# Expert phase: routed rows that are already normalised, results added to stored residuals, first layer in two-part weights

## The chip, the cores and the metric

One Trainium2 chip, one of its cores. The time is device microseconds for one execution of the program. The kernel before takes 1367.52 us (median of 3 runs, 1367.41 to 1367.99).

## The reference

The input `x` has 32 x 256 = 8192 tokens of 128 channels. Two sublayers follow each other. Each normalises its input (mean and variance over the channels, epsilon 1e-5, no scale), computes, normalises the result in the same way and adds it to its input.

```
x = x + layernorm(attention(layernorm(x)))       # 16 heads of 64, causal, 256 tokens, low-rank keys and values
x = x + layernorm(experts(layernorm(x)))         # 8 experts, each token to one of them

experts(f):  e     = argmax(f @ centroids.T)
             alpha = sigmoid(f . centroids[e])
             h     = (f - mean(f)) * rsqrt(var(f) + 1e-5) * gamma[e] + beta[e]
             y     = f + relu(h @ W1[e].T + b1[e]) @ W2[e].T + b2[e]     # 128 -> 512 -> 128
             out   = alpha * y + (1 - alpha) * f  =  f + alpha * (relu(...) @ W2[e].T + b2[e])
```

## The kernel before

Five engines run their own instruction lists and meet in semaphores; the order of the work on each is written out by hand.

**Attention** works in slots (`slot` and `phases`). A slot handles one pair of heads of one block of 256 tokens, 8 slots a block, 32 blocks. Matrices are kept in two parts, a high and a low one of type fp32r, and a product is three products of parts. ScalarE copies a result from PSUM as the high part, VectorE subtracts to get the low part (t, p, z). Beside the heads, slots carry steps for a whole block, by their place r = 0 to 7 in the block: for the block before, r 0 and 1 normalise the attention output and add the residual (x1), r 2 computes the statistics of x1 and its normalised form fn, r 3 turns fn, r 4 multiplies with the centroids, r 5 takes the argmax, r 6 computes each token's destination row, and r 7 scatters the rows. GpSimd does most of the block's small arithmetic. After the last block comes a drain of 16 slots (`not live(0)`), in which the last two blocks go through these steps.

**Routing.** A row in the DRAM tensor `routed_rows` has 136 numbers: x1 (128), the factor and shift that make fn from it, a second reciprocal deviation (of fn, for the experts' own normalisation), the best score, and the token's number. Every expert has its own region. In drain slot 6 SP and ScalarE each store four pads of 512 rows behind the regions (L224, in `pad`), with token numbers that lie outside the output. In drain slot 7 ScalarE multiplies the eight experts' first layer weights by gamma (L749). VectorE then computes a table: which expert and which rows each tile has.

**Experts** (`ffn_phases`, the functions `ffn_...`). 40 tiles of 256 rows, each of one expert, in a software pipeline: a prologue of 8 slots, a loop of 4 x 8, 5 slots of epilogue. For a tile, in order: SP loads the rows (`fin`); VectorE makes f (`ff`, L367) and its normalised form (`nn`, L375); TensorE turns it (L273), ScalarE copies it (`nt`, L310); TensorE multiplies by the first layer (L257, four blocks in fp32, in the profile two passes each); ScalarE adds the bias and relus two blocks (L317), VectorE two (L384); TensorE multiplies by the second layer (L283); ScalarE adds the bias (`yt`, L324); TensorE turns back (L266); VectorE forms f + alpha y (`gg`, L402) and its statistics (L408, L418); GpSimd takes the reciprocal deviation (L440, L442); VectorE normalises (`on`, L393); GpSimd adds x1 (`res`, L436) and scatters it to the output by two indirect DMAs (L446). ScalarE copies a tile's weights and biases, 1029 numbers a partition, into one of four buffers (L302) and computes exp(-score) (L305), of which VectorE makes alpha (L413, L422). A buffer of loaded rows is free again when the tile's scatters have landed.

Of the kernel before, what the change touches and what calls it, by code (L numbers as in the profile page):

```python
# [5 lines left out]
ALU = mybir.AluOpType  # L6
ACT = mybir.ActivationFunctionType
# [7 lines left out]
P = 128  # L15
# [4 lines left out]
C_RSTD = 128  # L20
C_SHIFT = 129
C_RSTD2 = 130
C_SCORE = 131
C_ID = 132
ROW = 136
# [4 lines left out]
def block_kernel(nc, x, wd_t, wup, wq_t, wo, cent_t, gamma_t, beta_t, ffn_w, out):  # L30
# [16 lines left out]
    TILES += -TILES % 8  # L47
# [4 lines left out]
    with ExitStack() as ctx:  # L52
# [6 lines left out]
        def sem(name):  # L59
# [53 lines left out]
        p_hi = sb("p_hi", [P, 2, 2, 384], F32R)  # L113
        p_lo = sb("p_lo", [P, 2, 2, 384], F32R)
# [7 lines left out]
        an = sb("an", [P, 2, P])  # L122
        pay = sb("pay", [P, 2, 2, ROW])
        st3 = sb("st3", [P, 2, 6])
        mv3 = sb("mv3", [P, 2, 2])
        ve3 = sb("ve3", [P, 2])
        w3 = sb("w3", [P, 3, 2])
        fn = sb("fn", [P, 2, P])
# [23 lines left out]
            dest_ready rows_written"""  # L152
# [3 lines left out]
        W1W = FB * P + FB  # L156
        WW = W1W + FB * P + 1
# [15 lines left out]
        fin = sb("fin", [P, FU, 2, ROW])  # L173
        ff = sb("ff", [P, FU, 2, P])
        nn = sb("nn", [P, 2, P])
        nt = sb("nt", [P, 2, T])
        wst = sb("wst", [P, 4, WW])
        assert 2 * HD == 2 * FB * T
        hid = wup_s[:].rearrange("p (b j t) -> p b j t", b=2, j=FB)
        yt = sb("yt", [P, T])  # L180
        ea = sb("ea", [P, FU, 2])
        ea1 = sb("ea1", [P, 2])
        alpha = sb("alpha", [P, FU, 2])
        gg = sb("gg", [P, 2, 2, P])
# [3 lines left out]
        gve = sb("gve", [P, 2])  # L188
        grs = sb("grs", [P, 2, 2])
        on = sb("on", [P, 2, P])  # L190
        res = sb("res", [P, 2, 2, P])
        for n in """pads_ready pad_stored ends_ready table_steps table_ready wst_ready exp_done nt_ready
            relu_a relu_d ff_done nn_ready n_tr h_done yt_done yt_ready y_tr alpha_steps g_steps gmv_ready gve_done
            grs_ready on_ready res_ready""".split():
            S[n] = sem(n)
# [10 lines left out]
        def ffn_phases(eng, slot):  # L206


            for s in range(FU):
                slot(0, 0, s, lambda lag: s >= lag)  # L210
# [5 lines left out]
            for s in range(5):  # L216
                slot(TILES, TILES // FU * 16, s, lambda lag: s < lag)
# [27 lines left out]
        def ffn_pe(pe):  # L245
            mm = nc.tensor.matmul

            def slot(m0, n0, s, live):
                if live(1):

                    pe.wait_ge(S["nt_ready"], m0 + s)
                    pe.wait_ge(S["wst_ready"], m0 + s)
# [886 lines left out]
```

## Time and profile before

| | us |
|---|---|
| median of 3 runs | 1367.52 |
| profiled execution | 1369.18 |
| its span, first to last instruction | 1366.2 |
| TensorE busy in the span | 1307.4 (96%) |
| VectorE | 1188.7 (87%) |
| ScalarE | 1082.8 (79%) |
| GpSimd | 908.9 (67%) |

The profile is of one execution. PE is TensorE's matmuls, PEld its weight loads, DVE is VectorE, ACT ScalarE, POOL GpSimd, SP SyncE; ACTq and SPq are what an engine's sequencer issues, DMAs for the most part. L12 is line 12 of the kernel. A matmul's end is modelled, so successive ones overlap in the rows and the distance of their starts is the better measure. Attention ends near 1130 us, the drain and the table at 1167, and the experts take the rest.

### The profile page before, as it was taken

The numbers are of one execution on the slowest core, as the hardware profiler recorded it, in microseconds if no ns is written. First come the engines' busy times: TensorE is split into PE (matmuls) and PEld (weight loads), VectorE is DVE, ScalarE is ACT, GpSimd is POOL, SyncE is SP. The second block draws the span as 40 slices with busy tenths as digits, with TensorE's granted clock in tenths as the row PEclk, the third lists the DMA queues.
The fourth block names the chain that finished last, engine by engine and source line by source line (L and its number), as shares of the span: only waits on it lengthen the run. The fifth ranks groups of instructions, "written<-read, shape, count | busy, mean of one in ns | idle before, by whom it ended". The sixth has DMA issues, their size and how long they took to land.

```text
span 1366.2 us, 34597 instructions
## 1 busy us (share of the span) xinstructions
PE 1307.4 (96%) x9120; PEld 1201.3 (88%) x9120; DVE 1188.7 (87%) x4712; ACT 1082.8 (79%) x3186; POOL 908.9 (67%) x1343
## 2 busy tenths in 40 slices
PE   6999999999999999999999999999999997699993
PEld 5999999999999999999999999999999996588782
DVE  4899999999999999999999999999999884699993
ACT  5988888888888888888888888888888884466661
POOL 3566666666666666666666666666666564288886
PEclk9999999999999999999999999999999998899997
DMA  5000000000000000000000000000000002122220
GB/s 211 5 9 13 12 12 12 12 12 12 12 12 12 12 12 12 12 12 12 11 9 8 11 12 12 12 12 12 12 12 8 8 10 76 42 62 59 60 61 8
DMA packets 38501, 31.83 MB, mean 23 GB/s; under 512 B 4882, under 2 KB 35734, under 8 KB 38080
## 3 DMA queue, kind: packets, MB, share of 16 engines
q1 hardware_dynamic: 31696, 21.47, 5.2%
q0 software_dynamic: 4656, 8.81, 1.9%
q10 hardware_dynamic: 2112, 1.11, 0.3%
q8 instruction: 16, 0.26, 0.1%
q14 instruction: 21, 0.17, 0.0%
HBM read 20.35 MB, written 12.07 MB: 24 GB/s over the span
## 4 chain that ended last, share of the span: by engine, by line
PE 82%; DVE 8%; issue 3%; POOL 3%; DMA 2%; ACT 1%; ACTq 0%; SPq 0%; POOLq 0%; DVEq 0%
PE psS L579 19%; PE psZU L643 13%; PE psZU L628 13%; PE psP L606 12%; PE psZU L631 7%; PE psT L595 5%; PE psT L597 4%; PE psT L596 4%; DVE ff L367 2%; DMA xin<-x 2%; DVE wup_s L384 1%; POOL out L446 1%; DVE on L393 1%; DVE gg L402 1%; PE psM L671 1%
## 5 line engine op out<-in xcount | busy, mean ns | idle before, releaser
L1097 POOL TENSOR_TENSOR prob<-prob,rinv 128x256 f32<-128x256 f32 (+1 forms) x512 | 412.9, 828 | 333.7 <-DVE rinv L858 330.4
L725 ACT ACTIVATE prob<-nscore,nmax 128x128 f32<-128x128 f32 (+1 forms) x1024 | 450.8, 445 | 3.1 <-DVE nmax L840 3.1
L840 DVE CUSTOM_DVE_ANT_0 nscore<-psS,mask 128x128 f32<-128x128 f32 (+1 forms) x1024 | 319.8, 349 | 0.2 <-PE psS L579 0.2
L697 ACT ACTIVATE t_hi<-psT 128x512 fp32r<-128x512 f32 x256 | 153.2, 598 | 151.3 <-PE psT L597 151.3
L827 DVE TENSOR_TENSOR t_lo<-psT,t_hi 128x512 fp32r<-128x512 f32 x256 | 176.5, 689 | 81.7 <-ACT t_hi L697 79.5
L849 DVE TENSOR_TENSOR p_lo<-psP,p_hi 128x768 fp32r<-128x768 f32 x256 | 243.3, 951 | 3.8 <-ACT p_hi L697 3.8
L697 ACT ACTIVATE p_hi<-psP 128x768 fp32r<-128x768 f32 x256 | 208.3, 814 | 6.3 <-PE psP L606 4.1
L606 PE MATMUL psP<-ident,prob 128*128 128x128 f32 x1536 | 209.3, 273 | 0.4 <-DVE p_lo L849 0.4
L863 DVE TENSOR_TENSOR z_lo<-psZU,z_hi 128x512 fp32r<-128x512 f32 x256 | 175.1, 684 | 28.4 <-ACT z_hi L697 14.4
L725 ACT ACTIVATION_READ_ACCUMULATOR prob<-nscore,nmax 128x1 f32 x1024 | 195.0, 190 | 0.0
L579 PE MATMUL psS<-t_lo,xt_hi 128*128 128x256 f32 (+1 forms) x512 | 194.3, 380 | 0.0
L606 PEld LDWEIGHTS psP<-ident,prob 128*128 128x128 f32 x1536 | 174.0, 141 | 0.6 <-issue 0.6
L579 PE MATMUL psS<-t_hi,xt_lo 128*128 128x256 f32 (+1 forms) x512 | 172.9, 338 | 0.0
L579 PE MATMUL psS<-t_hi,xt_hi 128*128 128x256 f32 (+1 forms) x512 | 172.6, 337 | 0.0
L595 PE MATMUL psT<-xt_hi,ab_lo 128*128 128x256 f32 x512 | 157.2, 307 | 2.0 <-DVE xt_lo L805 1.2
L697 ACT ACTIVATE z_hi<-psZU 128x512 fp32r<-128x512 f32 x256 | 148.1, 578 | 1.2 <-PE psZU L631 1.2
L643 PE MATMUL psZU<-z_hi,ab_lo 128*128 128x256 f32 x512 | 145.9, 285 | 0.0
L597 PE MATMUL psT<-xt_hi,ab_hi 128*128 128x256 f32 x512 | 143.8, 281 | 0.0
L596 PE MATMUL psT<-xt_lo,ab_hi 128*128 128x256 f32 x512 | 143.5, 280 | 0.0
L643 PE MATMUL psZU<-z_hi,ab_hi 128*128 128x256 f32 x512 | 143.4, 280 | 0.0
L643 PE MATMUL psZU<-z_lo,ab_hi 128*128 128x256 f32 x512 | 142.6, 279 | 0.0
L579 PEld LDWEIGHTS psS<-t_hi,xt_hi 128*128 128x128 f32 x512 | 96.4, 188 | 11.1
(168 smaller groups left out, 3295.7 us busy)
## 6 DMA issues: line engine op xcount, KB each, us to landing
fin<-routed_rows SPq DMA_DIRECT2D x40, 136.0 KB, 2.2
wx<-ffn_w SPq DMA_DIRECT2D x2, 2058.0 KB, 11.7
xin<-x SPq DMA_DIRECT2D x32, 128.0 KB, 2.2
xres<-x SPq DMA_DIRECT2D x32, 128.0 KB, 2.1
out<-res,fin POOLq DMA_INDIRECT x80, 2.3
routed_rows<-padr ACTq DMA_DIRECT2D x4, 272.0 KB, 4.3
routed_rows<-padr SPq DMA_DIRECT2D x4, 272.0 KB, 5.2
wup_s<-wup SPq DMA_DIRECT2D x1, 1024.0 KB, 5.0
```

Source lines behind the costliest of these rows:

```text
L579: last = mm(psQ[q], xx[:, xb, q * P:(q + 1) * P], tt[:, tb, :, 0:nk], start=(n == 0), stop=(n == 2))
L595: mm(psT[:, h, :], ab_lo[:, hh, 0, :], xt_hi[:, db, :], start=True, stop=False)
L596: mm(psT[:, h, :], ab_hi[:, hh, 0, :], xt_lo[:, db, :], start=False, stop=False)
L597: last = mm(psT[:, h, :], ab_hi[:, hh, 0, :], xt_hi[:, db, :], start=False, stop=True)
L606: last = nc.tensor.transpose(psP[:, h, k * P:(k + 1) * P], prob[:, s % 4, h, k * P:(k + 1) * P], ident[:])
L628: mm(psZ[:, :, :], xx[:, zx, 0, :], pp[:, zb, :, 0:T], start=(n == 0), stop=False, skip_group_check=True)
L643: last = mm(psU[:, 0:T], bb[:, hh, 1, :], zz[:, ub, h, :], start=(ur == 0 and h == 0 and n == 0), stop=(ur == PAIRS - 1 and h == 1 and n = ...
L697: cp = lambda o, i: nc.scalar.activation(o, i, ACT.Copy)
L725: last = nc.scalar.activation(prob[:, pb, h, a:z], nscore[:, (s - lag) % 2, h, a:z], ACT.Exp, bias=nmax[:, pb, h, q:q + 1], scale=-1.0, ac ...
L840: last = v.tensor_tensor_reduce(nscore[:, n1, h, a:z], psQ[q][:, h, :], mask[:, a:z], -1.0, -MASKED, ALU.add, ALU.min, nmax[:, p1, h, q:q ...
L849: v.tensor_tensor(p_lo[:, s % 2], psP[:, :, 0:384], p_hi[:, s % 2].bitcast(F32), ALU.subtract).then_inc(S["p_split"], 1)
L1097: last = g.tensor_tensor(pr, pr, rinv[:, p2, :, q:q + 1].broadcast_to([P, 2, z - a]), ALU.mult)
```

## The change

- A routed row has 132 numbers: the expert's normalised input (fn times its second reciprocal deviation), a gain (that deviation times alpha), an epsilon (the deviation squared times 1e-5), and the token's number. The expert phase works on results scaled by this deviation; its last normalisation takes the scaled epsilon, so the scale drops out. Alpha is computed in attention's slots (exp on ScalarE and two operations on VectorE at r 6), the multiplications are on GpSimd at r 4 and r 7.
- x1 is stored to the output by SP at r 2; the expert phase scatters only its normalised result, with an adding DMA. The addition `res` goes, and ff, nn and alpha's steps go from the expert phase. TensorE turns the loaded rows directly.
- First layer weights (times gamma) and the turned rows are in a high and a low part of type fp32r, and a block is three products. The weights are split in drain slots 1 to 8, high part on ScalarE, low part on VectorE; the eight scalings in slot 7 go. ScalarE copies each tile's two-part first layer (1024 numbers a partition), second layer (512) and biases (5) apart.
- 39 tiles instead of 40. The output normalisation, the scatter and the output side on VectorE come one slot later than before; buffers of the expert phase lie in those of attention, so its loads and copies wait for the last `z_ready`.

A line that only one of the two versions has is marked; of the old lines most stand in the functions above.

```diff
-C_RSTD = 128
-C_SHIFT = 129
-C_RSTD2 = 130
-C_SCORE = 131
-C_ID = 132
-ROW = 136
+C_GAIN = 128
+C_EPS = 129
+C_ID = 130
+ROW = 132
...
+        FIN = FU * 2 * ROW
+        fin = late[:, 0:FIN].rearrange("p (f t c) -> p f t c", f=FU, t=2)
+        gg = late[:, FIN:FIN + 4 * P].rearrange("p (b t c) -> p b t c", b=2, t=2)
+        nt_hi = sb("nt_hi", [P, 2, T], F32R)
+        nt_lo = sb("nt_lo", [P, 2, T], F32R)
+        w1 = sb("w1", [P, E, 2, FB * P], F32R)
+        w1st = p_both[:].rearrange("p m b h k -> p (m b h k)")[:, 0:4 * FB * P].rearrange(
+            "p (b m f) -> p b m f", b=2, m=2)
+        w2st = kv_t[:].rearrange("p (b m) j c -> p b (m j c)", b=2).rearrange("p b (m f) -> p (b m) f", m=2)
+        biases = sb("biases", [P, E, FB + 1])
+        bst = sb("bst", [P, 4, FB + 1])
...
+            n = TILES // FU
+            for s in range(FU):
+                slot(n * FU, n * 16, s, lambda lag: s - lag < rest)
+            for s in range(rest + 6 - FU):
+                slot((n + 1) * FU, (n + 1) * 16, s, lambda lag: s + FU - lag < rest)
...
+                    sp.wait_ge(S["z_ready"], PAIRS * NB)
...
+                    b = (s - 1) % 2
                     for j in range(FB):
-                        last = mm(psH[:, j, :], wst[:, (s - 1) % 4, j * P:(j + 1) * P], nt[:, (s - 1) % 2, :],
-                                  start=True, stop=True)
+                        for n, (m, nt) in enumerate(((1, nt_hi), (0, nt_lo), (0, nt_hi))):
+                            last = mm(psH[:, j, :], w1st[:, b, m, j * P:(j + 1) * P], nt[:, b, :],
+                                      start=(n == 0), stop=(n == 2))
...
+                    pe.wait_ge(f_loaded[s], n0 + 16)
...
+                        last = nc.tensor.transpose(psN[:, t * P:(t + 1) * P], fin[:, s, t, 0:P], ident[:])
...
+                    pe.wait_ge(S["w2st_ready"], m0 + s - 1)
...
+                if live(3):
+                    act.wait_ge(S["yt_done"], m0 + s - 2)
+                    if live(4):
+                        act.wait_ge(S["y_tr"], m0 + s - 3)
+                    nc.scalar.activation(yt[:], psY[:, 0, :], ACT.Identity,
+                                         bias=bst[:, (s - 3) % 4, FB:FB + 1]).then_inc(S["yt_ready"], 1)
                 if live(0):
-
+                    e = act.value_load(table[0:1, bass.ds(m0 + s, 1), 1], min_val=0, max_val=E - 1)
+                    if live(2):
+                        act.wait_ge(S["h_done"], m0 + s - 1)
+                    nc.scalar.activation(w1st[:, s % 2].rearrange("p m f -> p (m f)"),
+                                         w1[:, bass.ds(e, 1)].rearrange("p a m f -> p (a m f)"),
+                                         ACT.Copy).then_inc(S["w1st_ready"], 1)
+                if live(1):
+                    act.wait_ge(S["h_done"], m0 + s)
+                    act.wait_ge(S["w2st_ready"], m0 + s)
+                    if live(3):
+                        act.wait_ge(S["yt_done"], m0 + s - 2)
+                    for j in range(2):
+                        last = nc.scalar.activation(hid[:, (s - 1) % 2, j, :], psH[:, j, :], ACT.Relu,
+                                                    bias=bst[:, (s - 1) % 4, j:j + 1])
+                    last.then_inc(S["relu_a"], 1)
+                if live(0):
+                    act.wait_ge(S["n_tr"], m0 + s + 1)
+                    cp = lambda o, i: nc.scalar.activation(o, i, ACT.Copy)
+                    cp(nt_hi[:, s % 2, :], psN[:, 0:T]).then_inc(S["nt_hi_done"], 1)
...
+                    cp(w2st[:, s % 4, :], wx[:, bass.ds(e, 1), W2:W2 + FB * P].rearrange("p a c -> p (a c)"))
+                    cp(bst[:, s % 4, :], biases[:, bass.ds(e, 1), :].rearrange("p a c -> p (a c)")
+                       ).then_inc(S["w2st_ready"], 1)
...
+                if live(4):
+
+                    b, sf = s % 2, (s - 4) % FU
+                    m = m0 + s - 4
+                    dve.wait_ge(S["y_tr"], m + 1)
+                    if live(6):
+                        dve.wait_ge(S["on_ready"], m - 1)
                     for t in range(2):
...
+                        last = v.scalar_tensor_tensor(gg[:, b, t, :], psO[:, t, 0:P], fin[:, sf, t, C_GAIN:C_GAIN + 1],
+                                                      fin[:, sf, t, 0:P], ALU.mult, ALU.add)
                     last.then_inc(S["g_steps"], 1)
...
+                if live(1):
+                    dve.wait_ge(S["h_done"], m0 + s)
+                    dve.wait_ge(S["w2st_ready"], m0 + s)
...
+                    for j in range(2, FB):
+                        last = v.tensor_scalar(hid[:, (s - 1) % 2, j, :], psH[:, j, :],
+                                               bst[:, (s - 1) % 4, j:j + 1], 0.0, ALU.add, ALU.max)
...
+                if live(5):
+                    b = (s - 5) % 2
+                    dve.wait_ge(S["grs_ready"], m0 + s - 4)
+                    if live(7):
+                        dve.wait_ge(stored[(s - 7) % FU], n0 + n0 + (32 if s >= 7 else 0))
+                    for t in range(2):
+                        last = v.tensor_scalar(on[:, b, t, :], gg[:, b, t, :], gmv[:, b, t, 0:1], grs[:, b, t:t + 1],
+                                               ALU.subtract, ALU.mult)
+                    last.then_inc(S["on_ready"], 1)
...
+                    dve.wait_ge(S["nt_hi_done"], m0 + s + 1)
+                    v.tensor_tensor(nt_lo[:, s % 2, :], psN[:, 0:T], nt_hi[:, s % 2, :].bitcast(F32),
+                                    ALU.subtract).then_inc(S["nt_ready"], 1)
...
+            pool.wait_ge(S["x1_stored"], 16 * NB)
...
+                    m, b, sf = m0 + s - 4, s % 2, (s - 4) % FU
+                    pool.wait_ge(S["gmv_ready"], m + 1)
+                    g.tensor_tensor(gve[:, b, :], gmv[:, b, :, 1], fin[:, sf, :, C_EPS], ALU.add).then_inc(S["gve_done"], 1)
+                    pool.wait_ge(S["gve_done"], m + 1)
+                    g.tensor_tensor(grs[:, b, :], gve[:, b, :], neg_half[:], ALU.pow).then_inc(S["grs_ready"], 1)
+                if live(5):
+                    m, b, sf = m0 + s - 5, (s - 5) % 2, (s - 5) % FU
+                    wait_apart(pool, S["on_ready"], m + 1)
                     for t in range(2):
                         g.indirect_dma_start(out, bass.IndirectOffsetOnAxis(
-                            ap=fin[:, sf, t, C_ID:C_ID + 1].bitcast(U32), axis=0), res[:, b, t, :], None,
-                            bounds_check=ntok - 1, oob_is_err=False).then_inc(stored[sf], 16)
+                            ap=fin[:, sf, t, C_ID:C_ID + 1].bitcast(U32), axis=0), on[:, b, t, :], None,
+                            bounds_check=ntok - 1, oob_is_err=False,
+                            compute_op=ALU.add).then_inc(stored[sf], 16)
...
+                if r == 2 and live_b(2):
+                    sp.wait_ge(S["x1_ready"], b0 + db - 1)
+                    sp.dma_start(out[bass.ds((b0 + db - 2) * T, T), :].rearrange("(t p) c -> p t c", p=P),
+                                 x1[:, db]).then_inc(S["x1_stored"], 16)
...
+                if not live(0) and 1 <= s <= E:
+                    act.wait_ge(S["ffnw_loaded"], 5 * 16)
+                    nc.scalar.activation(w1[:, s - 1, 0, :], wx[:, s - 1, 0:FB * P], ACT.Copy,
+                                         scale=gam[:, s - 1:s]).then_inc(S["w1_hi_done"], 1)
...
+                if r == 6 and live_b(2):
+                    act.wait_ge(S["argmax_steps"], 3 * (b0 + db) - 5)
+                    nc.scalar.activation(ea[:], best[:], ACT.Exp, scale=-1.0).then_inc(S["exp_done"], 1)
...
-                if not live(0) and s == 7:
-
-                    act.wait_ge(S["bias_done"], E // 2 + 1)
-                    for e in range(E):
-                        last = nc.scalar.activation(wx[:, e, 0:FB * P], wx[:, e, 0:FB * P], ACT.Copy,
-                                                    scale=gam[:, e:e + 1])
-                    last.then_inc(S["weights_ready"], 1)
...
+                if not live(0) and 1 <= s <= E:
+                    dve.wait_ge(S["w1_hi_done"], s)
+                    v.scalar_tensor_tensor(w1[:, s - 1, 1, :], wx[:, s - 1, 0:FB * P], gam[:, s - 1:s],
+                                           w1[:, s - 1, 0, :].bitcast(F32), ALU.mult,
+                                           ALU.subtract).then_inc(S["w1_split"], 1)
...
-                    n = b0 + db - 1
-                    dve.wait_ge(S["r3_steps"], 6 * n - 4)
-                    v.scalar_tensor_tensor(pay[:, db, :, C_SHIFT], mv3[:, :, 0], -1.0, pay[:, db, :, C_RSTD],
-                                           ALU.mult, ALU.mult)
...
+                if r == 6 and live_b(2):
+
+                    dve.wait_ge(S["exp_done"], b0 + db - 1)
+                    v.tensor_scalar(ea1[:], ea[:], 1.0, None, ALU.add).then_inc(S["alpha_steps"], 1)
+                    dve.wait_ge(S["alpha_steps"], 2 * (b0 + db) - 3)
+                    v.reciprocal(alpha[:], ea1[:]).then_inc(S["alpha_steps"], 1)
...
+                    g.tensor_tensor(x1[:, db], an[:], xres[:, db], ALU.add).then_inc(S["x1_ready"], 1)
...
+                if r == 4 and live_b(2):
+
+                    n = b0 + db - 1
+                    wait_apart(pool, S["f_ready"], n)
+                    g.tensor_tensor(pay[:, db, :, 0:P], fn[:], rstd2[:].unsqueeze(2).broadcast_to([P, 2, P]),
+                                    ALU.mult).then_inc(S["nn_stored"], 1)
+                    g.tensor_tensor(sq2[:], rstd2[:], rstd2[:], ALU.mult).then_inc(S["gain_steps"], 1)
+                    pool.wait_ge(S["gain_steps"], 2 * n - 1)
+                    g.tensor_tensor(pay[:, db, :, C_EPS], sq2[:], eps_t[:], ALU.mult).then_inc(S["gain_steps"], 1)
...
+                    n = b0 + db - 1
+                    pool.wait_ge(S["alpha_steps"], 2 * n)
+                    g.tensor_tensor(pay[:, db, :, C_GAIN], rstd2[:], alpha[:], ALU.mult).then_inc(S["gain_ready"], 1)
+                    wait_apart(pool, S["dest_ready"], n)
+                    pool.wait_ge(S["gain_ready"], n)
+                    pool.wait_ge(S["nn_stored"], n)
+                    pool.wait_ge(S["gain_steps"], 2 * n)
```

## Rows read from the trace of the kernel before

**Rows 1.** Busy time by stretch: us, each engine's busy us (instructions), clock, DMA
```profile
60.00:1120.00 1060.00, 1059.53 (x7753) 990.28 (x7752) 959.35 (x3782) 910.14 (x2765) 713.56 (x1052) 1.00 0.04 11
1167.35:1172.13 4.78, 0.69 (x2) 0.29 (x2) 2.22 (x10) 1.49 (x3) 0.00 (x0) 0.50 0.35 89
1196.74:1336.39 139.65, 135.38 (x661) 112.28 (x660) 136.08 (x562) 90.51 (x198) 119.47 (x166) 1.00 0.20 60
```

**Rows 2.** Timeline of TensorE, experts: start us, us, what, idle before
```profile
1172.13 3.34 PE L257 MATMUL psS<-nt,wst 128*128 128x256 f32 x8 [0.47 <-ACT nt L310]
...
1272.68 1.89 PE L257 MATMUL psS<-nt,wst 128*128 128x256 f32 x8
1274.41 0.38 PE L266 MATMUL psZU<-ident,yt 128*128 128x128 f32 x2
1274.68 0.44 PE L273 MATMUL psZU<-ident,nn 128*128 128x128 f32 x2
1274.96 1.89 PE L283 MATMUL psT<-wup_s,wst 128*128 128x256 f32 x8
...
1336.39 1.89 PE L257 MATMUL psS<-nt,wst 128*128 128x256 f32 x8
```

**Rows 3.** Groups, 1196.74 to 1336.39: busy us, mean ns of one, idle before
```profile
L446 POOL DMA_INDIRECT out<-res,fin x67 | 67.2, 1003 | 17.5 <-issue 15.0 <-DVE on L393 2.4
L302 ACT ACTIVATE wst<-wx 128x1029 f32 x33 | 35.1, 1062 | 11.8 <-ACT yt L324 11.8
L384 DVE TENSOR_SCALAR wup_s<-psS,wst 128x256 f32<-128x256 f32 x66 | 28.7, 476 | 0.2
L367 DVE TENSOR_SCALAR ff<-fin 128x128 f32<-128x128 f32 x66 | 26.2, 437 | 1.0 <-issue 1.0
L436 POOL TENSOR_TENSOR res<-on,fin 128x256 f32<-128x256 f32 x33 | 24.6, 746 | 0.4
L393 DVE TENSOR_SCALAR on<-gg,gmv,grs 128x128 f32<-128x128 f32 x66 | 20.7, 366 | 0.0
L375 DVE TENSOR_SCALAR nn<-ff,fin 128x128 f32<-128x128 f32 x66 | 15.9, 283 | 1.2
```

**Rows 4.** Timeline between the phases
```profile
1146.37 0.49 DVE L785 BATCH_NORM_STATS2 st<-psM 128x6 f32<-128x128 f32 x2
1147.22 5.87 ACTq L224 DMA_DIRECT2D routed_rows<-padr  x4
...
1149.38 0.21 POOL L975 TENSOR_TENSOR ve<-mv,eps_t 128x2 f32<-128x2 f32 x1
...
1153.13 5.01 ACT L749 ACTIVATE wx<-wx,gam 128x512 f32<-128x512 f32 x8 [8.16 <-issue]
...
1158.04 0.36 ACT L697 ACTIVATE ft<-psM 128x256 f32<-128x256 f32 x1
...
1167.35 32.39 SPq L240 DMA_DIRECT2D fin<-routed_rows  x10
```

**Rows 5.** Chain of waits, attention: start us, us, what
```profile
1082.12 0.70 PE psZU L643 x6
```

**Rows 6.** Groups, 60 to 1130 us
```profile
L935 DVE SCALAR_TENSOR_TENSOR pay<-mv,pay 128x2 f32<-128x2 f32 x30 | 25.1, 836 | 0.0
L805 DVE TENSOR_TENSOR xt_lo<-psM,xt_hi 128x256 fp32r<-128x256 f32 x29 | 11.3, 391 | 0.0
```

**Rows 7.** Timeline of VectorE, attention, slot after r 6
```profile
635.91 0.69 DVE L827 TENSOR_TENSOR t_lo<-psT,t_hi 128x512 fp32r<-128x512 f32 x1 [0.28 <-ACT t_hi L697]
```

**Rows 8.** Timeline of GpSimd in the tail
```profile
1338.80 1.03 POOL L446 DMA_INDIRECT out<-res,fin  x1 [0.20 <-issue]
...
1356.92 0.98 POOL L446 DMA_INDIRECT out<-res,fin  x1 [0.30 <-issue]
```

**Rows 9.** DMA issues: number, KB each, us to landing
```profile
fin<-routed_rows SPq DMA_DIRECT2D x40, 136.0 KB, 2.2
out<-res,fin POOLq DMA_INDIRECT x80, 2.3
```

More of the change, by code:

```diff
@@ L126, in block_kernel @@
         ve3 = sb("ve3", [P, 2])
+        rs3 = sb("rs3", [P, 2])
         w3 = sb("w3", [P, 3, 2])
+        rstd2 = sb("rstd2", [P, 2])
+        sq2 = sb("sq2", [P, 2])
+        best = sb("best", [P, 2])
+        ea = sb("ea", [P, 2])
+        ea1 = sb("ea1", [P, 2])
+        alpha = sb("alpha", [P, 2])
         fn = sb("fn", [P, 2, P])
@@ L172, in block_kernel @@
         table = sb("table", [P, TILES, 2], I32)
[L173 to L178, printed above, removed]
+        late = prob[:].rearrange("p a h k -> p (a h k)")
+        FIN = FU * 2 * ROW
[9 more added lines that the diff above has]
+        bst = sb("bst", [P, 4, FB + 1])
+        assert 2 * HD == 2 * FB * T and HD // P == 2 * FB
         hid = wup_s[:].rearrange("p (b j t) -> p b j t", b=2, j=FB)
         yt = sb("yt", [P, T])
[L181 to L184, printed above, removed]
         gst = sb("gst", [P, 2, 6])
@@ L187, in block_kernel @@
         gmv = sb("gmv", [P, 2, 2, 2])
-        gve = sb("gve", [P, 2])
+        gve = sb("gve", [P, 2, 2])
         grs = sb("grs", [P, 2, 2])
[L190 to L194, printed above, removed]
+        on = sb("on", [P, 2, 2, P])
+        for n in """pads_ready pad_stored ends_ready table_steps table_ready w1_hi_done w1_split w1st_ready w2st_ready
+            nt_hi_done nt_ready relu_a relu_d n_tr h_done yt_done yt_ready y_tr g_steps gmv_ready gve_done
+            grs_ready on_ready""".split():
             S[n] = sem(n)
@@ L272, in slot @@
                     for t in range(2):
-                        last = nc.tensor.transpose(psN[:, t * P:(t + 1) * P], nn[:, t, :], ident[:])
+                        last = nc.tensor.transpose(psN[:, t * P:(t + 1) * P], fin[:, s, t, 0:P], ident[:])
                     last.then_inc(S["n_tr"], 1)
@@ L281, in slot @@
                     for j in range(FB):
-                        a = W1W + j * P
-                        last = mm(psY[:, 0, :], wst[:, (s - 2) % 4, a:a + P], hid[:, s % 2, j, :],
+                        last = mm(psY[:, 0, :], w2st[:, (s - 2) % 4, j * P:(j + 1) * P], hid[:, s % 2, j, :],
                                   start=(j == 0), stop=(j == FB - 1))
@@ L378, in slot @@
-                if live(1):
-                    dve.wait_ge(S["h_done"], m0 + s)
-                    if live(3):
-                        dve.wait_ge(S["yt_done"], m0 + s - 2)
-                    w = wst[:, (s - 1) % 4, :]
-                    for j in range(2, FB):
-                        last = v.tensor_scalar(hid[:, (s - 1) % 2, j, :], psH[:, j, :],
-                                               w[:, FB * P + j:FB * P + j + 1], 0.0, ALU.add, ALU.max)
-                    last.then_inc(S["relu_d"], 1)
@@ L387, in slot @@
-                if live(4):
-                    b = s % 2
-                    dve.wait_ge(S["grs_ready"], m0 + s - 3)
-                    if live(5):
-                        dve.wait_ge(S["res_ready"], m0 + s - 4)
-                    for t in range(2):
-                        last = v.tensor_scalar(on[:, t, :], gg[:, b, t, :], gmv[:, b, t, 0:1], grs[:, b, t:t + 1],
-                                               ALU.subtract, ALU.mult)
-                    last.then_inc(S["on_ready"], 1)
@@ L396, in slot @@
-                if live(3):
-                    b, sf = (s - 3) % 2, (s - 3) % FU
-                    m = m0 + s - 3
-                    dve.wait_ge(S["y_tr"], m + 1)
-                    for t in range(2):
-                        last = v.scalar_tensor_tensor(gg[:, b, t, :], psO[:, t, 0:P], alpha[:, sf, t:t + 1],
-                                                      ff[:, sf, t, :], ALU.mult, ALU.add)
+                if live(4):
[4 more added lines that the diff above has]
+                        dve.wait_ge(S["on_ready"], m - 1)
+                    for t in range(2):
+                        last = v.scalar_tensor_tensor(gg[:, b, t, :], psO[:, t, 0:P], fin[:, sf, t, C_GAIN:C_GAIN + 1],
+                                                      fin[:, sf, t, 0:P], ALU.mult, ALU.add)
@@ L921, in misc_early @@
                     b1v = wx[:, :, B1:W2]
-                    v.tensor_tensor(b1v, psT[:, 0, 0:E * FB].rearrange("p (e j) -> p e j", e=E), b1v,
+                    v.tensor_copy(biases[:, :, FB:FB + 1], wx[:, :, W2 + FB * P:W2 + FB * P + 1])
+                    v.tensor_tensor(biases[:, :, 0:FB], psT[:, 0, 0:E * FB].rearrange("p (e j) -> p e j", e=E), b1v,
                                     ALU.add).then_inc(S["bias_added"], 1)
```

106 lines of the change are left out of this document (22 added, 84 removed).

## The prediction

> **What bounds the kernel now.** I read the busy time by stretch first [rows 1]. Until 1120 us TensorE is busy 1059.53 of 1060.00 us: attention is TensorE's. In the steady part of the expert phase, 33 tiles from 1196.74 to 1336.39, one tile takes 139.65/33 = 4.23 us, and of it TensorE is busy 4.10, VectorE 4.12, GpSimd 3.62 and ScalarE 2.74. Three engines are near the end of the tile, so faster matmuls alone would give little. TensorE's own floor is read from one tile in which it never stopped [rows 2]: first layer 1.73 (1272.68 to 1274.41), two pairs of transposes 0.27 and 0.28, second layer 1.73, together 4.01. GpSimd's 3.62 is not all: the group of scattering DMAs shows 17.5 us of idle time before 67 of them, 0.53 a tile [rows 3], so it is bound for 4.15. Third, the timeline between the phases [rows 4]: 1142 to 1172 is a chain of small steps with TensorE nearly idle.
>
> **Steady expert tile.** First layer: eight fp32 passes in 1.73 become 12 fp32r products. Six products of this kind with changing weights take 0.70 [rows 5], so 12 x 0.118 = 1.42, and TensorE's floor falls by 0.31 to 3.70. VectorE loses ff and nn (26.2 + 15.9 us over 33 tiles, 1.28 a tile [rows 3]) and two small operations on alpha; it gains the low half of the turned rows, 0.39 by the same subtraction in attention [rows 6]: at most 4.12 - 1.28 + 0.39 = 3.23. GpSimd loses the residual addition: 4.15 - 0.75 = 3.40. ScalarE gains a copy of the second layer's weights, half of the 1029-wide copy's 1.06 [rows 3], and its exponential becomes a copy of five biases: 2.74 + 0.53 = 3.27. So TensorE becomes the floor, if the ring holds: from the start of a first layer, 1.42 + about 0.2 of release, then on VectorE two reluing halves (2 x 0.476), the two output normalisations (2 x 0.366), and the low half (0.39), which the next first layer waits for: 3.69, equal to TensorE's 3.70. ScalarE's reluing, high half and copies run beside that. I take 3.75; bounds 3.70 and 4.0 (the ring with collisions on top).
>
> **Number of tiles.** 39 instead of 40: 38 intervals between the first and the last first layer, where there were 39 in 1336.39 - 1172.13 = 164.26 [rows 2]. The granted clock is 0.50, the 1.2 GHz level, while TensorE is nearly idle before the first tile [rows 1], and the first of the intervals is stretched by that: 1.42 x 3.34/1.73 = 2.74 [rows 2], release 0.2, reluing 0.95, low half with release 0.6: 4.5. The second has no output transposes: 3.4. The others: 36 x 3.75 = 135.0. Another 1.0 for loop edges, which a TensorE without slack now pays. 143.9: **-20.4**.
>
> **Attention.** Each 256-token block gains on GpSimd one 128x256 multiply (the addition of this size is 0.746 [rows 3]) and three tiny ones, some 1.5 us where GpSimd is busy 713.56 of 1060 [rows 1]; on ScalarE one tiny exponential; on VectorE two tiny operations (some 0.3 with their waits) ahead of z_lo in slot 6 of the block, and it loses the two-input operation on L935, which shows 836 ns [rows 6]. SP gains a 128 KB store behind a wait for x1_ready that its next load waits for anyway. Against the 0.3 stands VectorE's idle 0.28 before the next t_lo [rows 7]; TensorE is the bound and has no wait there. I take 0. Bounds: -1 (some hidden waits on VectorE go) and +8 (0.25 in each of 30 blocks if that cover fails).
> L935 alone shows a mechanism: 836 ns for 128x2 elements that run beside GpSimd's normalisation. The Trainium skill (GPSIMD Engine Reference, Specifications) says that GpSimd shares its SBUF interfaces with VectorE and contends with instructions that have two SBUF inputs. By that rule the new weight split, two SBUF inputs as well, could wait once for a GpSimd operation in the drain, where VectorE has the time: the sum stays, within 0.8.
>
> **Between the phases.** Here I expect a loss. ScalarE's sequencer is held by the pad stores for 5.87 us from 1147.22 [rows 4]; until now nothing on VectorE waited for what comes behind them. Now ScalarE's seventh high-half copy (drain slot 7) is queued behind the pads, and VectorE's low half of it stands first in VectorE's slot 7, ahead of the statistics of the last attention output. Those began at 1146.37. Now: pads until 1153.1, the 512-wide copy 0.7, the split 0.7, statistics and aggregation 0.85: 1155.4. GpSimd took the result at 1149.38, since its scatter was in its way: +6.1. Behind it all is serial: GpSimd rs2, an, x1, fn, transpose. Back comes that ft was held by the eight weight scalings (ft at 1158.04, could be 1156.5): -1.5. The last block's alpha adds two operations before the table and a multiply before the last scatter: +0.8. First load of rows at 1167.35 + 5.4: **+5.4**. Bounds: -1.5 (no such wait) and +7.
>
> **Load to first layer.** 4.78 until now. ff and nn go (1.17), the low half comes (0.5): **-0.6**.
>
> **Tail.** From the start of the last first layer to the end of the last scatter it was 1357.90 - 1336.39 = 21.5 [rows 2, 8], paced by GpSimd. Now the first of five pairs of scatters is ready after 1.42 + 0.2 + 0.95 + 0.73 = 3.3, three more tiles at 3.40, then two pairs end on end at 2.5 each: 18.5. An adding scatter reads before it writes; landing is 2.3 now [rows 9], and I take 0.5 more: **-2.5**, bounds -3 and +2.
> The profile's row has plain stores only. The Trainium skill (DMA: Bandwidth & Descriptors, Rules for kernel authors) says that an accumulating DMA reads its destination and writes it later. By that rule, with the 2.2 of a load [rows 9] put on top of the 2.3, the tail alone would be 1.7 longer than in my sum, and the rows that are freed would still be in time.
> How much landing is free: the second scatter of a tile goes out some 4.5 us into its slot, and the load that reuses its rows needs 3.1, all within three slots and 1.7: up to 3 x 3.75 + 1.7 - 4.5 - 3.1 = 5.3.
>
> **Sum.** -20.4 + 5.4 - 0.6 - 2.5 = -18.1. The profiled execution took 1369.18 for a span of 1366.2; the median of the runs is 1.66 lower, so the sum is taken from the median: 1367.52 - 18.1 = **1349.4**.
>
> **Rivals.**
> A. The wait behind the pads doesn't reach the path: 1349.4 - 6.1 = 1343.3. For it: waits of several steps hide in each other there. Against: both queues are in order, and the profile shows ScalarE idle behind the pads.
> B. The steady tile stays near 4.0, as ring, ScalarE and GpSimd collide: 36 x 0.25 = +9.0, 1358.4. For it: four engines between 3.2 and 3.75 with a wait at each handing over. Against: TensorE was 4.10 busy of 4.23 with three engines as full.
> C. Attention pays 0.25 in each block: 1357.
> D. Slower: issuing the adding scatter holds GpSimd longer than the plain one's 1.0 [rows 3]. GpSimd's tile is 3.40 and grows by twice what one issue grows; TensorE's 3.75 hides 0.17 of it. The gain of 18.1 over 36 tiles is used up at a tile of 4.25, which is an issue of 1.43. At 1.6 a tile is 4.6: 36 x 0.85 + 5 in the tail = +35, 1385. For it: no row shows such a scatter. Against: the addition needs no more indices or rows.
>
> **Chances.** Forecast 0.55, A 0.10, B 0.17, C 0.08, D 0.10 (in a part of D it stays within the gain). Range: down to 1341 (A, with tiles at 3.70), up to 1361 (B with a slower landing); D is left out. A change of 0.2% (2.7 us) is what can be told from none here. Faster 0.88, within it 0.03, slower 0.09.
>
> **What would show it.** First layer: 12 products in 1.42. Steady first layers 3.7 to 3.8 apart with TensorE without idle time. VectorE's statistics in the drain at about 1155, with the low half of slot 7 waiting for ScalarE ahead of them; first load of rows near 1172.7. The adding scatter at 1.0 of GpSimd. I am wrong if that issue is over 1.2, if the steady tile is over 3.9, or if the drain's wait isn't there.

## The result: slower, 1385.84 us, and where the time went

The changed kernel takes 1385.84 us (median of 4 runs, 1384.52 to 1388.91), the kernel before 1367.76 beside it: ratio 1.0134, 95% interval 1.0115 to 1.0152. It was forecast at 1349.4, in a range up to 1361. The profiled execution took 1385.37 for a span of 1383.6.

The span grew by 17.4 us. Four stretches make it up, each between two rows that both timelines have (the first load of routed rows, the first and the last start of a first layer, the end):

| stretch | before | after | difference | forecast |
|---|---|---|---|---|
| start to first load of rows | 1167.35 | 1173.66 | +6.3 | +5.4 |
| first load to first first layer | 4.78 | 3.97 | -0.8 | -0.6 |
| first to last first layer | 164.26 | 170.77 | +6.5 | -20.4 |
| last first layer to the end | 29.8 | 35.2 | +5.4 | -2.5 |

Busy time by stretch of the kernel after, as [rows 1] (us, then each engine's busy us, granted clock, DMA share, GB/s):

```profile
60.00:1120.00 1060.00, 1058.03 (x7737) 988.94 (x7736) 955.05 (x3805) 907.74 (x2794) 743.27 (x1169) 1.00 0.05 15
1173.66:1177.63 3.97, 0.69 (x2) 0.29 (x3) 0.42 (x1) 1.71 (x3) 0.00 (x0) 0.50 0.44 96
1200.00:1340.00 140.00, 121.59 (x733) 100.57 (x733) 95.31 (x367) 99.95 (x212) 122.21 (x121) 1.00 0.42 55
```

In the expert phase VectorE has become light (95.31 of 140, where it had 136.08 of 139.65) and TensorE has idle time (121.59). GpSimd is the fullest, and its groups show that it is full to the end (busy us, mean ns of one, idle before):

```profile
L439 POOL DMA_INDIRECT out<-on,prob x61 | 95.9, 1572 | 15.7 <-issue 15.7
L432 POOL TENSOR_TENSOR gve<-gmv,prob 128x2 f32<-128x2 f32 x30 | 23.3, 778 | 0.0
```

The adding scatter holds it 1572 ns, where the plain one held it 1003 [rows 3]. With 15.7 us of "issue" (its own sequencer, nobody else) it is occupied for 122.21 + 15.7 = 137.9 of 140. One tile in GpSimd's timeline, and then the next:

```profile
1276.24 1.59 POOL L439 DMA_INDIRECT out<-on,prob  x1 [0.20 <-issue]
1278.13 1.55 POOL L439 DMA_INDIRECT out<-on,prob  x1 [0.30 <-issue]
1279.14 0.78 POOL L432 TENSOR_TENSOR gve<-gmv,prob 128x2 f32<-128x2 f32 x1
1280.00 0.72 POOL L434 TENSOR_TENSOR grs<-gve,neg_half 128x2 f32<-128x2 f32 x1
1280.91 1.59 POOL L439 DMA_INDIRECT out<-on,prob  x1 [0.20 <-issue]
```

1280.91 - 1276.24 = 4.67 us, and no other engine is waited for in it. TensorE's first layers follow at that pace, 4.64 apart on average between 1200 and 1310 us (the second to seventh interval were still 3.4 to 3.8; the first scatter goes out only at 1196.8). The waits of the others say the same only indirectly (us in total, times, longest):

```profile
DVE on L413 <- DMA out<-on,prob: 27.4, 29, 1.6
PEld psZU L285 <- DMA prob<-routed_rows: 18.0, 26, 1.0
PEld psS L269 <- DVE nt_lo L418: 12.9, 24, 1.6
```

Read alone, they accuse the landing of the scatter and the load of rows behind it. Both are possible readings, so the first experiments had to separate a slow issue (GpSimd's own time for the instruction) from a slow landing (the time until the data are written and the buffer is free).

### The profile page after: what moved, and what is told of

It reads as the page before. It is cut to its first block and busy times, and to the rows that moved or that the text cites. A ratio compares the mean times of both kernels' runs of the same rounds, so it can differ in the third digit from the quotient of the medians.

```text
span 1383.6 us, 34964 instructions
## 1 busy us (share of the span) xinstructions
PE 1296.3 (94%) x9256; PEld 1193.4 (86%) x9256; DVE 1151.7 (83%) x4541; ACT 1100.1 (80%) x3251; POOL 959.1 (69%) x1428
## 3 DMA queue, kind: packets, MB, share of 16 engines
q0 software_dynamic: 13328, 8.68, 4.5%
q10 hardware_dynamic: 2112, 1.08, 0.4%
## 5 line engine op out<-in xcount | busy, mean ns | idle before, releaser
L847 DVE TENSOR_TENSOR p_both<-psP,p_both 128x768 fp32r<-128x768 f32 x256 | 243.7, 952 | 1.2 <-ACT p_both L695 1.1
L695 ACT ACTIVATE p_both<-psP 128x768 fp32r<-128x768 f32 x256 | 208.1, 813 | 4.0 <-PE psP L604 2.4
L861 DVE TENSOR_TENSOR z_lo<-psZU,z_hi 128x512 fp32r<-128x512 f32 x256 | 174.6, 682 | 27.6 <-ACT z_hi L695 18.5
L626 PE MATMUL psZU<-p_both,xk_hi 128*128 128x512 f32 x512 | 160.7, 394 | 0.0
```

Source lines behind the costliest of these rows:

```text
L626: mm(psZ[:, :, :], xx[:, zx, 0, :], pp[:, zb, :, 0:T], start=(n == 0), stop=False, skip_group_check=True)
L695: cp = lambda o, i: nc.scalar.activation(o, i, ACT.Copy)
L847: v.tensor_tensor(p_lo[:, s % 2], psP[:, :, 0:384], p_hi[:, s % 2].bitcast(F32), ALU.subtract).then_inc(S["p_split"], 1)
L861: v.tensor_tensor(z_lo[:, (s - 5) % 2], psZ[:], z_hi[:, (s - 5) % 2].bitcast(F32), ALU.subtract).then_inc(S["z_split"], 1)
```

## The experiments

**1. The scatter without the addition.** The output then lacks the stored residuals.

```
-                            bounds_check=ntok - 1, oob_is_err=False,
-                            compute_op=ALU.add).then_inc(stored[sf], 16)
+                            bounds_check=ntok - 1, oob_is_err=False).then_inc(stored[sf], 16)
```

> The changed kernel with the last scatter storing instead of adding (the output then lacks the stored residual). Issue theory: the adding scatter holds GpSimd 1.57 us against 1.00 of the plain one, and with two of them a tile is 4.67 long on GpSimd; without it each issue is back at 1.0, GpSimd's tile at 3.5, the steady tile at TensorE's 3.7 to 3.8 and the time at 1350 (-36 from 1385.8). Landing theory (the read before the write makes the scatter land late, and the output normalisation waits for it): the same 1350, since it lands early again. If adding has nothing to do with it (the ring over VectorE is the limit, or the loads of rows): the tile stays at 4.5 to 4.7, 1380 to 1386.

1357.32 us, ratio 0.9917 (0.9899 to 0.9935). One attribute is worth 28.5 us. GpSimd's timeline with the plain scatter:

```profile
1282.95 1.04 POOL L439 DMA_INDIRECT out<-on,prob  x1 [0.19 <-issue]
1284.29 0.98 POOL L439 DMA_INDIRECT out<-on,prob  x1 [0.30 <-issue]
1285.26 0.29 POOL L432 TENSOR_TENSOR gve<-gmv,prob 128x2 f32<-128x2 f32 x1
1285.63 0.72 POOL L434 TENSOR_TENSOR grs<-gve,neg_half 128x2 f32<-128x2 f32 x1
1286.54 1.04 POOL L439 DMA_INDIRECT out<-on,prob  x1 [0.20 <-issue]
```

3.59 where nothing waits, 1.08 less than 4.67. But the tiles came on average 3.95 apart, not at 3.7 to 3.8, and the time is 7 us over the expected 1350: GpSimd waited for VectorE's normalised output (12.3 us in 130), VectorE for TensorE (18.4). Both theories had forecast the same 1350, so this run shows that adding is the cause but not by which of the two ways.

**2. Four result buffers instead of two**, so that VectorE waits for the scatter of three tiles before, not two. Where the buffer is written and scattered, its index goes over four as well (not shown).

```
-        on = sb("on", [P, 2, 2, P])
+        on = sb("on", [P, 4, 2, P])
...
-                    if live(7):
-                        dve.wait_ge(stored[(s - 7) % FU], n0 + n0 + (32 if s >= 7 else 0))
+                    if live(8):
+                        dve.wait_ge(stored[s % FU], n0 + n0)
...
```

> The changed kernel with four buffers of results for the scatters instead of two: the output normalisation waits for the scatter of three tiles before, not of two. Issue theory: VectorE's wait for a landing gets short or goes, but GpSimd issues at the same pace, tile 4.67, time 1384 to 1387. Landing theory: the tile falls to 3.8 to 4.1, 1355 to 1365.

1387.99 us, ratio 1.0138 (1.0121 to 1.0155); tiles 4.63 apart. That is 1 us above the issue theory's range and far from the landing theory's. The wait that the list put first was given room and is gone from the list, and nothing came of it: it is not the bound. The loads of rows still wait for landings here (14.7 us in 110 in the kernel after, 22.5 here), so the landing as such is left to run 3.

**3. The square root's chain off GpSimd**, the scatter still adding.

```
-                    g.tensor_tensor(gve[:, b, :], gmv[:, b, :, 1], fin[:, sf, :, C_EPS], ALU.add).then_inc(S["gve_done"], 1)
...
-                    g.tensor_tensor(grs[:, b, :], gve[:, b, :], neg_half[:], ALU.pow).then_inc(S["grs_ready"], 1)
...
+                    v.tensor_tensor(gve[:, b, :], gmv[:, b, :, 1], fin[:, sf, :, C_EPS], ALU.add).then_inc(S["gve_done"], 1)
...
+                    nc.scalar.activation(rt[:, s % 2, :], gve[:, s % 2, :], ACT.Sqrt).then_inc(S["rt_done"], 1)
...
+                    v.reciprocal(grs[:, b, :], rt[:, b, :]).then_inc(S["grs_ready"], 1)
```

> The changed kernel, still adding, with the reciprocal deviation taken off GpSimd (addition and reciprocal on VectorE, square root on ScalarE). Issue theory: GpSimd's tile falls from 4.67 by its two small operations (about 0.95) to 3.75, the steady tile to 3.8 to 3.9, the tail by 3, time 1351 to 1356. Landing theory: the scatters go out no more often than they land, tile 4.5 to 4.7, time 1380 to 1386.

1358.68 us, ratio 0.9923 (0.9906 to 0.9939): 27.2 less, though 3 us above the expected range. Two small operations are gone from GpSimd, and the tiles come 3.82 apart. The scatter adds as it did, its issue is 1.56 us, and still no wait for a scatter's landing is in the list any more, and TensorE's weight loads wait for rows 1.4 us in 110 instead of 14.7. TensorE is now busy 108.44 of 110 us. GpSimd's time was the bound, and the waits for landings followed from it.

**4. The kernel before with nothing but the addition** in its scatter (it adds onto an output that nobody has filled).

> The kernel before with one word changed: its last scatter adds to the output (what it adds to is undefined; all else is as it was). Issue theory: GpSimd's tile grows from 4.15 by 2 x 0.57 to 5.3, each of 39 intervals by 1.07: +42, 1410. Landing theory: only the wait for the scatter of two tiles before could grow, by about 1 us beyond its slack: under +10.

1417.96 us in one run. GpSimd's tile there:

```profile
1284.37 1.59 POOL L446 DMA_INDIRECT out<-res,fin  x1 [0.20 <-issue]
1286.26 1.54 POOL L446 DMA_INDIRECT out<-res,fin  x1 [0.30 <-issue]
1287.26 1.30 POOL L436 TENSOR_TENSOR res<-on,fin 128x256 f32<-128x256 f32 x1
1287.98 0.73 POOL L440 TENSOR_TENSOR gve<-gmv,eps_t 128x2 f32<-128x2 f32 x1
1288.79 0.72 POOL L442 TENSOR_TENSOR grs<-gve,neg_half 128x2 f32<-128x2 f32 x1
1289.70 1.66 POOL L446 DMA_INDIRECT out<-res,fin  x1 [0.20 <-issue]
```

5.33 a tile on GpSimd, where it was 4.15 busy and issuing in the kernel before. So a kernel with nothing else of the change pays too, +48.5 us: 41.6 between the first and the last first layer (forecast +42), and 6.4 in the tail, which the forecast had left out. It belongs to the addition, not to how it meets the new order.

**5. The splitting of weights earlier in the drain**, so that it is over before ScalarE's pad stores. The table gives for each slot the weights split in it; ScalarE's and VectorE's half both go by it, with i for s - 1.

```
+        def split_at(s, live):
+            return {1: (0,), 2: (1,), 3: (2, 3), 4: (4, 5), 5: (6,), 6: (7,)}.get(s, ()) if not live(0) else ()
...
-                if not live(0) and 1 <= s <= E:
+                for i in split_at(s, live):
...
```

> The changed kernel, with the splitting of the eight first-layer weights placed earlier in the drain of the attention phase, so that ScalarE and VectorE have done all eight before ScalarE comes to its pad stores. The adding scatter is untouched. Theory 1 (the wait of VectorE's last low half behind ScalarE's pad stores is what makes the first load late, 1167.35 -> 1173.66 us): the first load comes at about 1168.5, 5 us sooner, and the time falls by 5, to 1380.5 us. Rival: the first load is late by the longer chain of the last blocks (exponential, reciprocal, gain product ahead of the last scatter of rows), and the split moves nothing: 1385, first load at 1173. A half result (2 to 3 us) would mean that both stand one behind the other.

1379.22 us, ratio 1.0074 (1.0059 to 1.0089): 6.6 less. The kernel after between the phases, as [rows 4]:

```profile
1148.84 5.53 ACTq L233 DMA_DIRECT2D routed_rows<-padr  x4
1154.41 1.33 ACT L730 ACTIVATE w<-wx,gam 128x512 fp32r<-128x512 f32 x2 [7.93 <-issue]
1155.16 0.75 DVE L917 SCALAR_TENSOR_TENSOR w<-wx,gam,w 128x512 fp32r<-128x512 f32 x1 [7.02 <-ACT w L730]
1155.83 0.49 DVE L783 BATCH_NORM_STATS2 st<-psM 128x6 f32<-128x128 f32 x2
1173.66 0.41 SPq L250 DMA_DIRECT2D prob<-routed_rows  x1
```

and with the earlier split:

```profile
1145.99 0.47 DVE L786 BATCH_NORM_STATS2 st<-psM 128x6 f32<-128x128 f32 x2
1146.78 5.23 ACTq L233 DMA_DIRECT2D routed_rows<-padr  x4
1149.62 0.21 POOL L983 TENSOR_TENSOR ve<-mv,eps_t 128x2 f32<-128x2 f32 x1
1166.13 3.83 SPq L250 DMA_DIRECT2D prob<-routed_rows  x4
```

The statistics stand ahead of the pads again, and the load of rows comes at 1166.13. To compare executions I take a mark that all of them have near the end of attention, six transposes of probabilities. Here it is in the kernel before, the kernel after and this run:

```profile
1109.41 0.82 PE L606 MATMUL psP<-ident,prob 128*128 128x128 f32 x6
1110.57 0.82 PE L604 MATMUL psP<-ident,prob 128*128 128x128 f32 x6
1108.51 0.82 PE L607 MATMUL psP<-ident,prob 128*128 128x128 f32 x6
```

This execution was 2.06 earlier by that mark (1108.51 against 1110.57), so the repair gave 7.53 - 2.06 = 5.5 us: the wait behind the pads was all of the loss here. The other runs agree: from the mark to the first load it is 57.6 to 58.2 in the kernel before and runs 4, 5, 6 and 9, and 62.7 to 63.2 in the kernel after and runs 1, 2, 3, 7, 8 and 10.

**6. Both repairs together**, 3 and 5.

> The changed kernel with both repairs: the splitting placed earlier as in the run before, and the square root's chain of the expert phase taken off GpSimd (add and reciprocal on VectorE, square root on ScalarE). If the two causes are independent, their gains add up: 1385.8 - 27.2 (measured for the second alone) - 5 = 1353.5 us, ratio to the kernel before 0.989. Rival: with the second alone the expert phase is bound by TensorE, whose clock falls back if it starts otherwise, or the earlier split costs the attention phase what it gives later: 1357 to 1359, no better than the second repair alone.

1351.64 us, ratio 0.9880 (0.9862 to 0.9899), over 6 runs: it beats both kernels, by 17 and 34 us. The gains add up (27.2 and 6.6). GpSimd and TensorE in its steady stretch:

```profile
1283.81 1.56 POOL L443 DMA_INDIRECT out<-on,prob  x1 [0.31 <-issue]
1285.68 1.56 POOL L443 DMA_INDIRECT out<-on,prob  x1 [0.30 <-issue]
1287.54 1.56 POOL L443 DMA_INDIRECT out<-on,prob  x1 [0.30 <-issue]
```

```profile
1283.08 0.39 PE L270 MATMUL psS<-nt_hi,p_both 128*128 128x256 f32 x1
...
1284.61 0.38 PE L279 MATMUL psZU<-ident,yt 128*128 128x128 f32 x2
1284.82 0.38 PE L286 MATMUL psZU<-ident,prob 128*128 128x128 f32 x2
1285.04 1.89 PE L296 MATMUL psT<-wup_s,kv_t 128*128 128x256 f32 x8
1286.78 0.39 PE L270 MATMUL psS<-nt_hi,p_both 128*128 128x256 f32 x1
```

Both show the same tile: two issues at 1.865 apart are 3.73, and TensorE goes round in 1286.78 - 1283.08 = 3.70. That is the most frequent distance; some tiles take longer, and the average from 1200 to 1310 us is 3.82.

**7. Half of the rows in each adding scatter** (64 of 128; the others get no result).

```
-                            ap=fin[:, sf, t, C_ID:C_ID + 1].bitcast(U32), axis=0), on[:, b, t, :], None,
+                            ap=fin[0:P // 2, sf, t, C_ID:C_ID + 1].bitcast(U32), axis=0), on[0:P // 2, b, t, :], None,
```

> The changed kernel, but each adding scatter takes 64 of the 128 rows of its half tile (the other 64 rows get no result: that part of the computation is left out). It tells what the issue's 1.57 us on GpSimd grows with. Issue by row (plain 1.00 for 128 rows; the addition writes a descriptor of its own for each row): about 0.8 to 1.0 us each, GpSimd's tile falls from 4.67 to 3.4 and the steady tile to TensorE's 3.8, time 1355 to 1360. Issue fixed by the instruction: still 1.5 us, tile 4.6, time 1385. The packets per issue tell too: 144 with 128 rows, 72 to 80 if they go by row.

1375.79 us in one run. It lies between the two expectations, nearer to the one of a fixed price (1385, with a tile of 4.6): the issue is 1439 ns, the tile 4.39.

```profile
L439 POOL DMA_INDIRECT out<-on,prob x50 | 71.9, 1439 | 12.4 <-issue 12.4
```

Only 0.13 of 1.57 went with half of the rows. If the rest of it grew evenly with rows, 0.27 would be for the rows and 1.3 for none of them; that is an estimate from two sizes. The packets did go by row. GpSimd's queue, after and here (packets, MB, share of 16 engines):

```profile
q0 software_dynamic: 13328, 8.68, 4.5%
```

```profile
q0 software_dynamic: 8336, 6.63, 3.0%
```

With the plain scatter the queue has 4592 packets in 142 issues, 32.3 each. The 64 scatters of the attention phase are plain in all of them (2070 packets), which leaves (13328 - 2070)/78 = 144 for an adding scatter of 128 rows and 80 for one of 64: one a row, and 16 more.

**8. Without the store of the residuals** in the attention phase (the output lacks them).

> The changed kernel without the store of the residuals into the output in the attention phase (the output then lacks them), nor the wait of GpSimd for it. It asks whether the attention phase's 1.2 us by the last block (psP of the last block 1100.84 -> 1102.00) and the rest up to 2.2 us come from these 32 transfers or from SyncE's wait ahead of them. If so: last normalisation at 1129.7 instead of 1131.1 and the time 1383.5 to 1384.5. Rival: they come from the added operations on GpSimd and VectorE (product of the row, gain, split of weights in the drain): nothing changes, 1385.5 and 1131.

1385.22 us in one run, last normalisation at 1129.45. The time fits the rival, the 1129.45 would fit the store's theory; but the run with the earlier split has the store and was sooner still, at 1129.06, and the kernel after had 1131.13. So where the phase ends moves by 2 us from one execution to the next, and the 0.6 us below the kernel after is too little to tell. Counted from the mark, the last normalisation comes 20.56 later with the store (kernel after) and 20.56 without it, and 20.29 in the kernel before: the store costs nothing there. No cost of the attention phase was found; one below 1 us stays open.

**9. Both repairs and a plain scatter** (the output lacks the stored residuals).

> The kernel with both repairs (split earlier, square root's chain off GpSimd), its scatter without the addition (the output then lacks the stored residuals). With the addition its steady tile is 3.71 us, in which GpSimd's two issues take 2 x (1.56 + 0.30) = 3.72 and TensorE is busy 108.1 of 110 us: which of the two is the bound? If TensorE: the tile stays at 3.70 to 3.75, and the time falls only by the shorter last scatters, 2 x 0.57 + about 1, to 1349.5 us. If GpSimd: the tile falls to about 3.6 and the time to 1345 or less.

1346.12 us, ratio 0.9831 (0.9813 to 0.9849): the time lies between the two expectations, 3.4 below TensorE's and 1.1 above GpSimd's. The trace says TensorE: it is busy 109.45 of 110 while GpSimd is busy 57.57, and the most frequent tile stays at 3.70. But the average falls from 3.82 to 3.76, so GpSimd at 3.73, right beside TensorE, had a small part as well. Adding costs that kernel 5.5 us still: 4.1 of it in the tail (31.1 against 27.0).

**10. Forty tiles instead of 39.**

```
+    TILES += -TILES % 8
```

> The changed kernel with the number of tiles rounded up to a multiple of eight again (40 instead of 39; the last one holds only pad rows). What the removed tile is worth: one steady tile of this kernel, 4.67 us, so 1390.5 us and a ratio to the kernel before of 1.017. Rival: a tile of pad rows goes nowhere, its scatters are issued but write nothing, and its issue may be shorter; then 2 to 4 us, 1388 to 1389.8.

1389.86 us, ratio 1.0160 (1.0143 to 1.0177): +4.0, where one tile at GpSimd's pace is 4.67. Its profiled span is 4.2 longer; the interval holds both theories. The trace is against the rival's reason: the last two issues, the pad tile's, are as long as any, and the queue has 288 packets more than in the kernel after, 144 for each of them.

```profile
1378.05 1.55 POOL L440 DMA_INDIRECT out<-on,prob  x1 [0.30 <-issue]
1379.90 1.54 POOL L440 DMA_INDIRECT out<-on,prob  x1 [0.30 <-issue]
```

This trace also has the landings of the adding scatters, which those of the kernel after and run 3 lack. Beside them the plain ones of run 9 (number of issues, us from issue to landing):

```profile
out<-on,prob POOLq DMA_INDIRECT x80, 3.3
out<-on,prob POOLq DMA_INDIRECT x78, 2.3
```

So an adding scatter does land 1.0 us later, 0.6 of which is its longer issue. Run 3 shows that this wasn't the bound.

## Why the prediction was wrong, step by step

- **Number of tiles and steady tile, -20.4: wrong by 26.9, the step that decided.** It failed in "GpSimd loses the residual addition: 4.15 - 0.75 = 3.40". This took the adding scatter at the plain one's 1.0; it takes 1.57, GpSimd's round is 4.67, and that instead of TensorE's 3.70 is the pace. Rival D had the mechanism and, at 1.6, the size (1385); what it got was 0.10, on the argument "the addition needs no more indices or rows". The argument doesn't hold: with the same indices and rows the issue is 1.57 instead of 1.00. No row showed such a scatter, and the whole gain hung on an issue below 1.43: an unseen operation on an engine with 0.35 us of room was no case for 0.10.
The Trainium skill (Perfetto Trace Analysis, DMA Instruction — SWDGE (GPSIMD)) says that for a DMA issued by GpSimd the profile's interval ends when the last descriptor is written, not when the data has moved. The runs agree that the 1.57 us is GpSimd's own time: four result buffers changed nothing, and taking two small operations off GpSimd, 0.94 us of its round of 4.67, took the whole loss away. They don't bear out that it is simply so much for each packet: from 144 to 80 packets takes off 0.13 us, and a plain scatter with 32 packets is another 0.43 below that. What GpSimd does in the fixed part stays open.
- **The same tile with an issue of 1.0** would not have been 3.75 but 3.95 (run 1): rival B, the collisions in the ring, was true as well. GpSimd's own round is 3.59 there, not 3.40. The square root's chain on GpSimd is part of the ring; with it gone, TensorE's 3.70 came out as the most frequent tile (runs 6 and 9), to the hundredth by luck, for its parts were a little off: first layer 1.53 instead of 1.42, the two pairs of transposes 0.21 and 0.22 instead of 0.27 and 0.28.
- **Filling, 4.5 and 3.4 for the first two intervals: right.** In the kernel after they were 4.59 and 3.36:

```profile
1177.63 0.58 PE L269 MATMUL psS<-nt_hi,p_both 128*128 128x256 f32 x1 [0.93 <-DVE nt_lo L418]
1182.22 0.39 PE L269 MATMUL psS<-nt_hi,p_both 128*128 128x256 f32 x1 [1.33 <-DVE nt_lo L418]
1185.58 0.40 PE L269 MATMUL psS<-nt_hi,p_both 128*128 128x256 f32 x1
```

The granted clock rose to the upper level within the first interval there (0.67 on average, then 1.00), and so it did in run 1. In runs 2, 3 and 5 to 10 it rose only during the second, which then took 4.7 to 5.5 us. The first three tiles of run 9:

```profile
1172.48:1177.07 4.59, 3.35 (x15) 2.95 (x15) 1.30 (x3) 2.94 (x9) 0.00 (x0) 0.50 0.49 122
1177.07:1182.49 5.42, 5.42 (x23) 5.05 (x23) 1.30 (x3) 2.76 (x8) 0.00 (x0) 0.57 0.11 27
1182.49:1186.09 3.60, 3.60 (x26) 3.36 (x25) 1.36 (x4) 3.04 (x7) 0.00 (x0) 1.00 0.00 0
```

The later rise took 5.42 - 3.36 = 2.1 us there. It doesn't look like the work of an edit: run 10, which only adds a tile at the end, had 5.39. It is a difference between executions as far as the runs show, and it explains most of why the 38 intervals of run 9, whose bound is the one forecast, are 146.4 and not 143.9: without the first two they are 136.4, forecast 136.0.
- **Attention, 0: right** as far as it can be told. TensorE was busy 1058.03 of 1060.00. The mark near its end stands between 1108.4 and 1110.6 in the ten executions of the changed attention (1109.4 on average, run 8 among them without the store), and at 1109.4 and 1110.0 in the two of the old one. Rival C is out.
- **Between the phases, +5.4: right, in place and size.** From the mark to the first load it was 57.9 before and 63.1 after, +5.2, and run 5 took 5.5 of it away. Statistics at 1155.83, forecast "at about 1155". Rival A is out. That a split could wait once for a GpSimd operation came true twice: the first two low halves on VectorE took 1.11 and 1.35 us beside GpSimd operations of 1.04, the other six 0.72 to 0.75. They stood at 1132 to 1137, where no loss shows, as forecast.
- **Load to first layer, -0.6:** -0.8.
- **Tail, -2.5: +5.4.** Again the issue. From the start of the last first layer to the end of the last scatter it was 28.8, forecast 18.5: the pairs went out at 4.67, not 3.40, and there were six and not five, since GpSimd was a tile behind. From there to the end of the span it was 6.4, where it was 8.3 before; why it is shorter stays open. With the plain scatter the tail was 27.9 (run 1) and 27.0 (run 9), which is -1.8 and -2.8. The 0.5 for a later landing was small but real: run 10 shows 1.0 from the start of the issue, 0.4 from its end.
- **D's price at 1.6 was +35 over the forecast; it came to +36.4.** The rival's mechanism was right; the close number has some luck in it, with a tail of 7.9 over the forecast where it had 5. The chance given to it was not sound.

## What to carry to other kernels

Before counting on an operation that no row of the trace shows, work out the price at which it eats the gain; if its engine is nearly full, as GpSimd was in this loop, give that case the weight of a real unknown, or time the one operation first (run 4 was one attribute). The plain scatter of 128 rows cost GpSimd 1.28 us from one issue to the next, the adding one 1.87: move small arithmetic off it before giving it one. And work that is moved next to a queue of stores must be looked at on both engines that it ties together: here two of eight weight splits stood behind it, and moving them was worth 5.5 us.

## What the runs showed of the hardware that was not expected

- An adding indirect scatter of 128 rows of 512 bytes holds GpSimd for 1.57 us where the plain one takes 1.00; issues end on end go out every 1.87 and 1.28 us. By the run with half of the rows (1.44) some 1.3 of the 1.57 doesn't depend on their number, an estimate from two sizes. A tile of pad rows cost the same issue (run 10, 1.54 and 1.55). It lands 3.3 us after the start of its issue (run 10), the plain one 2.3 (run 9).
- It makes 144 packets for 128 rows and 80 for 64, the plain one 32 for 128. The queue's packets took 4.5% of the DMA engines' span instead of 1.9%. The DMA engines were not the bound: their busy share from 1200 to 1310 us was 0.41 in the kernel after and 0.50 in run 3, which was 27 us faster.
- GpSimd's small operation behind an adding scatter shows 0.78 us (`gve`) instead of the 0.20 to 0.35 behind a plain one. Its record starts 1.0 after the scatter's start and so overlaps the scatter's 1.55. The likely reading, not tested, is that it is longer by waiting; only the distance from issue to issue is a price.
- The granted clock rose at different places in executions of nearly the same order of work: within the first expert tile in the kernel after and run 1 (second interval 3.36 and 3.34 us), only during the second in eight other runs (4.66 to 5.50), in which TensorE had no idle time either.
